# A fused image-and-text transformer layer: the last 64 channels of token rows and expert weights held once, with weights packed to 128 lanes

## The reference

```python
h = _L0_tok_ref(x, W, b, cls_token, pos_embed)        # patches @ W + b, class token, positions
h = jnp.concatenate([h, txt], axis=1)                  # 1 + 196 + 77 = 274 tokens
h = h + _L0_attn_ref(_layernorm(h), ...)               # 12 heads of 16, rotary, causal
h = h + _L0_ffn_ref(_layernorm(h), ...)

def _ffn(x, W1, b1, W2, b2):
    return jax.nn.gelu(x @ W1 + b1, approximate=False) @ W2 + b2     # 192 -> 768 -> 192
common = _expert_mix(h, route_c, W1c, ...) * scale_c   # 4 experts, the best one per token
unique = _expert_mix(h, route_u, W1u, ...) * scale_u   # 4 more
out = common + dropped[:, None] * unique               # tokens over an expert's capacity
```

## Time and profile before

| | |
|---|---|
| median of three runs | 1414.29 us (1412.52 to 1417.49) |
| the profiled execution | 1427.62 us |
| its span, first to last instruction | 1425.9 us |
| mean granted TensorE clock | 0.933 |
| PE busy | 1234.0 us (87%) |
| weight loads busy | 1049.4 us (74%) |
| DVE, ACT, POOL busy | 906.9, 560.0, 628.5 us |
| HBM read and written | 129.15 and 50.38 MB |
| the expert half | 938 to 1426 us |

### The profile page before, as it was taken

The page is one execution under the profiler, slowest core; times in us unless marked ns, Lnnn a source line. Parts: engine busy times, 40 slices in busy tenths (PEclk is TensorE's granted clock), DMA queues, the critical chain, the costliest instruction groups (busy, mean ns, idle before and its releaser), DMA issues.

```text
span 1425.9 us, 33277 instructions
## 1 busy us (share of the span) xinstructions
PE 1234.0 (87%) x12722; PEld 1049.4 (74%) x12722; DVE 906.9 (64%) x2063; ACT 560.0 (39%) x959; POOL 628.5 (44%) x996
## 2 busy tenths in 40 slices
PE   6889999999999999999999987468995788889874
PEld 4667777777777777777777775367994787789874
DVE  5676776786787777787777874567873343445331
ACT  1234334434444344344344343133552344455430
POOL 4133333334534534534534525415325465455564
PEclk8899999999999999999999998579996899889987
DMA  6001211213323313213323223477764566657530
GB/s 204 20 20 48 69 39 58 63 58 100 111 60 107 106 58 111 99 61 104 108 59 106 86 61 109 144 292 271 254 236 126 168 213 208 220 207 271 203 127 26
DMA packets 84368, 177.93 MB, mean 125 GB/s; under 512 B 16446, under 2 KB 57701, under 8 KB 84208
## 3 DMA queue, kind: packets, MB, share of 16 engines
q1 hardware_dynamic: 70544, 146.93, 31.8%
q0 software_dynamic: 13664, 28.84, 5.7%
HBM read 129.15 MB, written 50.38 MB: 126 GB/s over the span
## 4 chain that ended last, share of the span: by engine, by line
PE 41%; DVE 21%; issue 15%; POOL 11%; ACT 6%; DMA 3%; another core or an unknown queue 1%; SPq 1%; POOLq 0%; DVEq 0%; ACTq 0%
PE y_ps L1629 9%; PE h_ps L1618 9%; DVE capped L971 4%; ACT PT L739 3%; PE round_banks L582 3%; PE gen L502 3%; POOL sorted_d L226 3%; DVE xn L987 3%; POOL PT L853 3%; PE gen L544 2%; PE round_banks L555 2%; DVE nm L975 2%; PE gen L511 2%; DVE nm L973 2%; PE gen L594 2%
## 5 line engine op out<-in xcount | busy, mean ns | idle before, releaser
L739 ACT ACTIVATE PT<-round_banks 128x1752 f32<-128x1752 f32 x96 | 156.7, 1632 | 176.0 <-PE round_banks L582 176.0
L853 POOL TENSOR_SCALAR_AFFINE_SELECT PT<-PT 128x512 f32<-128x512 f32 x192 | 118.1, 640 | 209.8 <-ACT PT L739 209.3
L1708 ACT ACTIVATE Gl<-h_ps,W 128x256 f32<-128x256 f32 x264 | 118.1, 474 | 233.1 <-PE h_ps L1618 147.8
L1618 PE MATMUL h_ps<-XH,Wh 128*128 128x256 f32 x528 | 155.4, 310 | 46.7 <-issue 29.9
L1629 PE MATMUL y_ps<-W,Gl 128*128 128x192 f32 x1056 | 193.2, 338 | 2.8 <-issue 2.8
L1629 PEld LDWEIGHTS y_ps<-W,Gl 128*128 128x128 f32 x1056 | 181.5, 199 | 4.9 <-issue 4.8
L1533 POOL DMA_INDIRECT out_dram<-Y,sid x88 | 95.5, 1085 | 154.3 <-DVE Y L1801 130.8
L502 PE MATMUL gen<-w_emb,xT 128*128 128x192 f32 (+1 forms) x768 | 142.9, 338 | 7.7 <-DMA ident<-in_ident_dram 7.7
L1618 PEld LDWEIGHTS h_ps<-XH,Wh 128*128 128x128 f32 x528 | 109.2, 207 | 50.9 <-issue 37.4
L1618 PE MATMUL h_ps<-XH,Wl 128*128 128x256 f32 x528 | 146.6, 297 | 0.0
L971 DVE TENSOR_TENSOR capped<-round_banks,masks_f 128x1024 f32<-128x1024 f32 x96 | 116.2, 1211 | 33.7 <-PE round_banks L555 33.7
(11 more groups left out here) (272 smaller groups left out, 2462.5 us busy)
## 6 DMA issues: line engine op xcount, KB each, us to landing
W<-in_experts_dram SPq DMA_DIRECT2D x44, 771.0 KB
W<-in_experts_dram SPq DMA_DIRECT2D x44, 672.0 KB
xT<-in_xT_dram SPq DMA_DIRECT2D x32, 591.0 KB
X<-sorted_d SPq DMA_DIRECT2D x35, 450.0 KB
stage<-rows_d SPq DMA_DIRECT2D x64, 224.0 KB
rows_d<-xn SPq DMA_DIRECT2D x32, 256.0 KB
rows_d<-h SPq DMA_DIRECT2D x32, 192.0 KB
out_dram<-h SPq DMA_DIRECT2D x32, 192.0 KB
```

The costliest lines, as they stand in the source:

```text
L739: act.activation(PT[(JG * b + j) % 2][:], R[:, :, 0:438], ACT.Exp, scale=SCALE).then_inc(exps, 1)
L853: pool.affine_select(x[:, :, at:at + P], x[:, :, at:at + P], [[0, GH], [1, P]], ALU.is_ge, 0.0, base=0, channel_multiplier=-1)
L1618: mm = pe.matmul(h_ps[f % 3][:, 0:ROWS], w[t.par][:, cols], x, start=(k == 0), stop=(k == len(products) - 1))
L1708: act.activation(Gl[t.par][:, f, :], h_ps[f % 3][:, 0:ROWS], ACT.Gelu, bias=W[t.i][:, B1O + f:B1O + f + 1]).then_inc(g_ready, 1)
```

## The change

The last 64 channels are kept once in a row: `DX` becomes 192, a row of `rows_d` has 384 columns (448 before) and one of `sorted_d` 386 (450). The second transpose of `turn` now takes channels 64 to 191, so lanes 64 to 127 hold the last channels and lanes 0 to 63 channels that are of no use there. DVE overwrites those lanes with the low part of the last channels, which it reads from lanes 64 to 127. The weights of the last channels are packed: lanes 0 to 63 hold their hidden columns 0 to 383, lanes 64 to 127 columns 384 to 767, so they take 384 columns instead of 768. ACT unpacks them while it rounds: one instruction for the first block and two that write the same 64 lanes to both halves of `Wh`. DVE makes `Wl` in two instructions, the last channels on lanes 64 to 127 alone. The fifth product of a group therefore takes lanes 64 to 127 alone, where before it took all 128.

```diff
-W1O, B1O, W2O, B2O = 0, 2 * FF, 2 * FF + FC, 2 * FF + FC + FC * D
+HF = FF // 2
+W1O, B1O = 0, FF + HF
+W2O, B2O = B1O + FC, B1O + FC + FC * D
-DX = 2 * P
+DX = D
...
-                    scale_twice(LN2, 0, xn2[b % 2][:, 0, :], h[b % 8][:, 0, :])
-                    scale_twice(LN2, 1, xn2[b % 2][:, 1, :], h[b % 8][:, 1, :]).then_inc(xn2_ready, 1)
+                    scale(LN2, 0, xn2[b % 2][:, 0, :], h[b % 8][:, 0, :])
+                    scale(LN2, 1, xn2[b % 2][:, 1, :], h[b % 8][:, 1, :]).then_inc(xn2_ready, 1)
...
+        upper = slice(D - P, P)
+        def first_rows(w, half):
+            return w[:, half * HF:(half + 1) * HF]
+        def last_rows(w, half):
+            return w[:, FF + half * HF:FF + (half + 1) * HF]
+        def packed(half):
+            return slice(half * (D - P), (half + 1) * (D - P))
...
-                    mm = pe.transpose(xt_ps[:, ROWS + k * P:ROWS + (k + 1) * P],
-                                      x[:, k, P:DX], eye[:])
+                    mm = pe.transpose(xt_ps[:, ROWS + k * P:ROWS + (k + 1) * P], x[:, k, D - P:D], eye[:])
...
-                    products = ((Wh, a, xa), (Wh, a, xl), (Wl, a, xa), (Wh, b, xb), (Wl, b, xb))
+                    high = XH[t.par][upper, ROWS:2 * ROWS]
+                    products = ((Wh[t.par][:, a], xa), (Wh[t.par][:, a], xl), (Wl[t.par][:, a], xa), (Wh[t.par][:, b], xb), (Wl[t.par][upper, b], high))
...
-                act.activation(halves(Wh[t.par], half), halves(W[t.i], half), ACT.Copy).then_inc(wh_ready, 1)
+                act.activation(first_rows(Wh[t.par], half), first_rows(W[t.i], half), ACT.Copy)
+                for copy in range(2):
+                    ins = act.activation(last_rows(Wh[t.par], half)[packed(copy)], W[t.i][packed(half), FF:B1O], ACT.Copy)
+                ins.then_inc(wh_ready, 1)
...
-                low, cols = slice(D - P, P), slice(ROWS, 2 * ROWS)
-                dve.tensor_tensor(XH[t.par][low, cols], xt_ps[low, cols], XH[t.par][low, cols], ALU.subtract).then_inc(xt_ready, 1)
+                low, high, cols = slice(0, D - P), slice(D - P, P), slice(ROWS, 2 * ROWS)
+                dve.tensor_tensor(XH[t.par][low, cols], xt_ps[high, cols], XH[t.par][high, cols], ALU.subtract).then_inc(xt_ready, 1)
...
-                dve.tensor_tensor(halves(Wl[t.par], half), halves(W[t.i], half), halves(Wh[t.par], half),
-                                  ALU.subtract).then_inc(wl_ready, 1)
+                dve.tensor_tensor(first_rows(Wl[t.par], half), first_rows(W[t.i], half), first_rows(Wh[t.par], half), ALU.subtract)
+                dve.tensor_tensor(last_rows(Wl[t.par], half)[upper], W[t.i][packed(half), FF:B1O],
+                                  last_rows(Wh[t.par], half)[packed(half)], ALU.subtract).then_inc(wl_ready, 1)
...
-        w[i, :, :, FF:B1O] = np.concatenate([w1[:, P:], w1[:, P:]], 1)
+        w[i, :, :, FF:B1O] = np.concatenate([w1[:, P:, 0:HF], w1[:, P:, HF:FF]], 1)
```

More of the change, by code:

```diff
@@ L987, in scale @@
                 return dve.tensor_scalar(dst, src, mv[:, which, k, 0:1], rstd[:, which, k:k + 1], ALU.subtract, ALU.mult)
-            def scale_twice(which, k, dst, src):
-                scale(which, k, dst[:, 0:P], src[:, 0:P])
-                twice = lambda x: x.rearrange("p (a d) -> p a d", d=D - P)
-                return scale(which, k, twice(dst[:, P:DX]), twice(src[:, P:D]).broadcast_to([P, 2, D - P]))
             def norm_tail(g):
@@ L1181, in _ @@
                     dve.wait_ge(rstd_ready[LN2T], g + 1)
-                    scale_twice(LN2T, 0, xn2t[:], ht[g % 4][:]).then_inc(xn2t_ready, 1)
+                    scale(LN2T, 0, xn2t[:], ht[g % 4][:]).then_inc(xn2t_ready, 1)
                 if t.mid is not None:
@@ L1395, in rows @@
             return late[t.i] if t.at_least(FIXED) else X[t.i]
-        def halves(w, half):
-            return w[:, 0:2 * FF].rearrange("p (c h f) -> p c h f", c=2, h=2)[:, :, half, :]
+        upper = slice(D - P, P)
[5 more added lines that the diff above has]
+            return slice(half * (D - P), (half + 1) * (D - P))
         @block.sync
@@ L1615, in up @@
                     xa, xl, xb = XH[t.par][:, 0:ROWS], XL[t.par][:], XH[t.par][:, ROWS:2 * ROWS]
-                    products = ((Wh, a, xa), (Wh, a, xl), (Wl, a, xa), (Wh, b, xb), (Wl, b, xb))
-                    for k, (w, cols, x) in enumerate(products):
-                        mm = pe.matmul(h_ps[f % 3][:, 0:ROWS], w[t.par][:, cols], x, start=(k == 0), stop=(k == len(products) - 1))
+                    high = XH[t.par][upper, ROWS:2 * ROWS]
+                    products = ((Wh[t.par][:, a], xa), (Wh[t.par][:, a], xl), (Wl[t.par][:, a], xa), (Wh[t.par][:, b], xb), (Wl[t.par][upper, b], high))
+                    for k, (w, x) in enumerate(products):
+                        mm = pe.matmul(h_ps[f % 3][:, 0:ROWS], w, x, start=(k == 0), stop=(k == len(products) - 1))
                     mm.then_inc(h_filled, 1)
```

## The result

The changed kernel takes 1444.2 us (median of four runs, 1442.73 to 1450.39), the kernel before in the same comparison 1415.89 us (1412.52 to 1420.47): a ratio of 1.0189, 95% interval 1.0152 to 1.0225. The change costs 28 us. It was forecast to cost 58.

The account below looks back on a forecast made before the run. TensorE was taken to set the pace of the steady expert tiles. +72 us for changes of shape, -8 for attention and -6 for bytes made +58 on 1427.6 us: 1486, carried to 1472 us, range 1430 to 1510.

Parts of the forecast that it names:

- The price of a change of shape: In `up` of each expert tile: 0.19 us per change, 12 changes, 2.28 us, so a tile takes 10.2 instead of 7.95 us.
- How much of it is on the path: Thirty tiles from 1022 to 1333 us: 28 pay the full 2.28 us, +64 us; two already wait for ACT.
- The stalls' cause: Slow stretch, 1064 to 1126 us: perhaps crowded transfers; smaller transfers were taken at -6 us, ends 0 and -30.
- The first eight tiles: Expert tiles from 938 to 1022 us: longer `up` first fills PE's waits for DVE, so +8 us, ends 0 and 18.
- the clock falls: Rival: PE's drains put `up` and transposes at half clock in half of 28 tiles, +63 us, 1535 us; chance 0.10.
- The attention half: Normalized rows written once, two DVE instructions instead of four per sequence: -8 us, ends +5 and -25.
- ACT's and DVE's roundings: Expert tiles: ACT rounds in three instructions, 1.4 us, DVE subtracts in two of 0.56 us; hidden in the steady tiles.
- The side estimate: Behind the third gelu: if changes of shape cost nothing, PE would wait for ACT some 0.5 us per tile.
- The carried difference: Whole kernel: the profiled execution lay 13.3 us over the median, so 1486 us became 1472 us.
- Only the drain is paid: Rival in `up`: half-row load pulled ahead or its exposure halved, 1.1 us per tile, +21 us, 1435 us; chance 0.10.
- low end: Whole kernel: 64 us, 0 in the first tiles, less 25 and 25 of the 30, +14: 1428, rounded to 1430 us.
- high end: Whole kernel: 28 x 2.5 + 18 + 9 + 0 = +97 us: 1511, rounded to 1510 us.

Follow-up runs that it names:

- eight products: Kernel before with the fifth product taken four times per group, no change of shape: 1434.13 us, ratio 1.0531 without stalls; 1479.26 us, 1.0440 with stalls.
- six changes: Changed kernel with every second group's products reversed, so 64-lane products stand side by side: 1402.7 us, ratio 1.0298; repeated 1397.79 without stalls, 1434.85 with.

## Why the prediction was wrong

*The price of a change of shape: right.* 0.186 against 0.19 us, tile 10.18 against 10.2, read from the changes into and out of 32 lanes. Full, six and no changes confirm it (tiles of 10.18, 9.07, 7.95). The Trainium skill ("TensorE: Matmul & The Clock Gate", Part 2), which I had set against it, has a weight load for the background buffer pulled ahead of running products. At a change of shape the trace does not agree: the 64-lane load starts 0.21 us behind the 128-lane product before it (1113.06 to 1113.27), and the 128-lane load 0.31 us behind the 64-lane product (1112.29 to 1112.60).

*How much of it is on the path: this step failed.* "In two of them, in the stretch of rows 4, PE stands between the groups for ACT anyway, so 28 x 2.28 = 64 us." I had read the windows of one quiet stretch, 1290 to 1330, and one disturbed one, 1064 to 1126, and took the rest as quiet. It wasn't: the thirty tiles held 71.6 us of excess, up to tile 31. The trace had it in plain view: one window over 1064 to 1333 shows PE idle for 46.7 us at a granted clock of 0.89, and thirty tiles in 310 us are 10.3 us each, not 7.95. Against 64 - 6 = +58 for these tiles stands +9.9: the price was paid in all thirty of them (66.9 us), and the excess of before shrank by 57.0. The step that failed is the overlap: the stalls of before were not subtracted. That they shrink is shown; that the added length does it is shown for a part only, since eight products of the same length kept 45 us of them.

*The stalls' cause: not seen.* I allowed only transfers that crowd each other, with 0 to 30 us. Scattered list writes set them off, and the shorter transfers give at most a part: the kernel with the fifth product on all lanes has all the savings in bytes and keeps 66.9 of 73.7 us of excess. Its -10 us in all are mostly the attention half, which ends 8 us earlier.

*The first eight tiles: sized too low, and a rival was right here.* +13.9 against +8. PE's wait for `part` of the earlier trace rows shrank from 9.6 to 2.8 us as expected. But the first two tiles alone are 11.7 us longer. Windows of the first `up`, after and then before:

```profile
929.11:939.04 9.93, 9.93 (x30) 7.24 (x30) 2.14 (x5) 3.72 (x8) 0.00 (x0) 0.50 1.00 402
```

```profile
938.73:943.81 5.08, 5.08 (x31) 5.08 (x31) 1.39 (x4) 2.55 (x6) 0.00 (x0) 0.69 1.01 406
```

Before, the products step by 0.21 us up to 941.85 and by 0.12 us from then on, in the middle of `up`; after, all of `up` runs at the lower level (granted clock 0.50), and so does the second one. All kernels with twelve changes per tile show it (`up` 9.4 us to the start of its last product, in tiles 0 and 1), while eight products without a change take 7.1 to 8.0. That is the rival "the clock falls", in two tiles and not in half of 28.

*The attention half: right here.* -9.6 against -8; in the profiles the first expert product starts at 929 to 932 us with the change in eight of ten kernels and at 935 to 941 without it in nine of ten; the exceptions (937.1 and 935.7 with, 930.9 without) show that the 8 us are not certain in a single execution. On the chips without stalls the gain does not reach the total (ratio 1.0006): why is open.

*ACT's and DVE's roundings: right in size and hidden.* 1.46 and 1.12 us per half. The side estimate that ACT would cost 0.5 us per tile if changes of shape were free is wrong.

*The carried difference* of the profiled execution from the median was right for before, and of no use for after, whose profiled execution lies 0.7 us under its median. That it brought the forecast nearer, from 1486 to 1472, is luck.

*The rivals.* None described it. "Only the drain is paid" gave 1435 us, nearer than my 1472, by a mechanism that the steps of 0.31 and 0.21 us exclude. The right rival would have been: the price is whole, and the stalls shrink by most of it. That 1444 us lies in the stated range of 1430 to 1510 is luck too: its low end was made of 25 us less in the attention half and 25 less by transfers, and neither came. The high end leaves out the +5 of the attention half.

## What to carry to other kernels

Before multiplying a price per tile by the number of tiles, divide the whole stretch by its tiles: what lies over the steady period is time that the change may shrink, and its cause has to be known before the price is charged. Here one way to lengthen the tile shrank it by 46 us and another by 18. A change of array shape between products of 256 columns in the faster 32-bit mode costs 0.19 us at full clock each way, so products of one shape belong side by side. And where two chips differ by 4% on the same kernel, a ratio from one of them is not the ratio of the change.

## What the runs showed of the hardware beyond that

- The same kernel takes 1360 us on three of the chips (1359.53, 1360.38, 1361.34) and 1416 to 1423 in the other three comparisons. Taking away 72 scattered writes of GpSimd (1.02 us each) and the wait for them brings both to 1346 to 1356 us. Why ACT, DVE and PE answer to them with late starts, and in some comparisons only, is open.
- At half clock a change of shape costs more. Kernel after, the timeline of PE, two groups:

```profile
1100.63 0.58 PE L1623 MATMUL h_ps<-XH,Wl 64*128 64x256 f32 x1
...
1102.29 0.58 PE L1623 MATMUL h_ps<-XH,Wl 64*128 64x256 f32 x1
```

  1.66 us per group; five steps of 0.213 us are 1.07, which leaves 0.30 us per change.
- A product on half of the lanes takes as long as on all: with six changes two of them and the way back take 0.43 us (1157.99 to 1158.42), with twelve one and the way back 0.31, so the second takes 0.12. So does a rounding on ACT (518 against 515 ns for 384 columns).
